# Two operands of a Mamba layer's gating moved into PSUM: the conv's Tanh, and y up to its gate

## The reference

```python
proj = h @ in_proj_w.T                       # h: layernorm(x)
gate, xBC, dt = split(proj, [INTER, INTER + CONV_DIM])
xBC = silu(causal_conv4(xBC) + conv_b)       # 4 taps, one filter per channel
x, Bm, Cm = split(xBC)
y = ssd(x, Bm, Cm, dt) + x * D               # mixing of tokens by C.B * decay, and the skip term
yg = y * silu(gate)
out = rmsnorm_by_group(yg) * norm_w @ out_proj_w.T
```

## Time and profile before

| | |
|---|---|
| median of 3 runs | 1576.83 us |
| the profiled execution's own time | 1575.93 us |
| its span, first to last instruction | 1573.70 us |
| mean granted TensorE clock | 0.993 of full speed |
| PE busy | 1529.4 us, 97% |
| DVE busy | 1367.7 us, 87% |
| POOL busy | 1045.9 us, 66% |
| ACT busy | 1010.5 us, 64% |

### The profile page before, as it was taken

One profiled execution on the slowest core, in us unless ns is written; L12 is line 12 of the kernel. 1 busy time (PEld: TensorE's weight loads), 2 busy tenths in 40 slices (PEclk: granted clock), 3 DMA queues, 4 the chain that ended last, 5 costly groups with the idle time before them and its releaser, 6 DMA issues. The chain is left out here.

```text
span 1573.7 us, 24488 instructions
## 1 busy us (share of the span) xinstructions
PE 1529.4 (97%) x8296; PEld 1229.0 (78%) x8296; DVE 1367.7 (87%) x1676; ACT 1010.5 (64%) x2126; POOL 1045.9 (66%) x789
## 2 busy tenths in 40 slices
PE   6978999999999999999999999999999999999988
PEld 4766788788888888788888888788888888788766
DVE  6679988998889988998889988998889988998674
ACT  4467766667666667667666667666666677567641
POOL 3026887588757887588757887488757886588740
PEclk9989999999999999999999999999999999999999
DMA  3033332223222232233222332223223322222101
GB/s 122 1 105 110 101 95 75 84 92 95 86 71 93 94 95 74 81 94 96 81 74 95 95 95 74 81 94 95 81 75 94 94 95 74 81 94 81 59 17 53
DMA packets 73514, 131.62 MB, mean 84 GB/s; under 512 B 10800, under 2 KB 10800, under 8 KB 73136
## 3 DMA queue, kind: packets, MB, share of 16 engines
q1 hardware_dynamic: 73392, 130.07, 25.9%
HBM read 127.43 MB, written 2.62 MB: 83 GB/s over the span
## 5 line engine op out<-in xcount | busy, mean ns | idle before, releaser
L164 PE MATMUL bank<-h_hi,mx_w_hi 128*128 128x512 f32 x1152 | 457.5, 397 | 5.1 <-DVE mx_xd L1480 4.0
L166 PE MATMUL bank<-h_hi,mx_w_lo 128*128 128x512 f32 x1152 | 449.5, 390 | 0.0
L165 PE MATMUL bank<-h_lo,mx_w_hi 128*128 128x512 f32 x1152 | 448.4, 389 | 0.0
L970 DVE SCALAR_TENSOR_TENSOR mx_acc<-bank,mx_cw,mx_acc 128x510 f32<-128x510 f32 (+2 forms) x480 | 353.7, 745 | 55.4 <-ACT mx_acc L955 43.9
L1289 ACT ACTIVATE mx_mix<-mx_csb,ncs 128x256 f32<-128x256 f32 x512 | 217.9, 497 | 138.5 <-PE bank L1679 138.5
L1473 DVE TENSOR_TENSOR mx_mix<-mx_mix,mx_cbt 128x1536 f32<-128x1536 f32 x128 | 280.5, 2196 | 2.5 <-ACT mx_mix L1299 2.5
L917 POOL TENSOR_TENSOR mx_w_lo<-mx_w_raw,mx_w_hi 128x512 fp32r<-128x512 f32 x144 | 213.8, 1501 | 74.3 <-ACT mx_w_hi L912 74.1
L164 PEld LDWEIGHTS bank<-h_hi,mx_w_hi 128*128 128x128 f32 x1152 | 216.5, 188 | 50.9 <-issue 8.7
L166 PEld LDWEIGHTS bank<-h_hi,mx_w_lo 128*128 128x128 f32 x1152 | 216.3, 188 | 46.3
L1200 POOL TENSOR_TENSOR mx_ssum<-mx_ssum,mx_sq 128x512 f32<-128x512 f32 x112 | 216.3, 1954 | 51.5 <-ACT mx_sq L1321 51.5
L165 PEld LDWEIGHTS bank<-h_lo,mx_w_hi 128*128 128x128 f32 x1152 | 216.7, 188 | 42.7
(11 more groups left out here) (171 smaller groups left out, 2132.6 us busy)
## 6 DMA issues: line engine op xcount, KB each, us to landing
mx_csb<-cs_rows SPq DMA_DIRECT2D x128, 512.0 KB, 3.9
mx_w_raw<-in_w_in SPq DMA_DIRECT2D x144, 256.0 KB, 2.9
mx_wo_raw<-in_w_out SPq DMA_DIRECT2D x64, 256.0 KB, 4.1
res<-in_x SPq DMA_DIRECT2D x8, 256.0 KB, 4.8
out<-res SPq DMA_DIRECT2D x8, 256.0 KB, 2.0
f_base_raw<-in_base_wt SPq DMA_DIRECT2D x1, 1024.0 KB, 7.4
mx_acc<-in_base_wt SPq DMA_DIRECT2D x1, 1024.0 KB, 4.8
cs_rows<-f_xn SPq DMA_DIRECT2D x2, 256.0 KB, 2.0
```

The lines of the kernel that those rows point to most:

```text
L164: nc.tensor.matmul(out, w_hi, x_hi, start=first, stop=False)
L165: nc.tensor.matmul(out, w_hi, x_lo, start=False, stop=False)
L166: return nc.tensor.matmul(out, w_lo, x_hi, start=False, stop=last)
L970: self.nc.vector.scalar_tensor_tensor(dst, src[:, :, 0:SEQ - k], self.cw[:, c, TAPS - 1 - k:TAPS - k], dst, ALU.mult, ALU.add).then_inc(s[ ...
```

## The change

1. `tanh_conv` writes its result into the projection's own bank (`m.bank[u % 2]`), no longer into the SBUF tile `th`, except for units 2 and 3; `silu_conv` reads it there. So the bank is in use until `silu_conv` of the unit is done, and `ip.project` waits on `conv` where it waited on `tap` (for units 0 to 3 and 6 onward; units 4 and 5, which follow 2 and 3, still wait on `tap`).
2. `skip_y` leaves its sum in `Y_BANK`. `gate_y` moves from POOL to DVE: it reads the bank and `sg` and writes `y` to SBUF, behind both `skip_y` of a pair. The mixing two steps later, and the next group's `b_dot_c`, wait on `yg` (gate done) where they waited on `ysb` (sum done). The wait on `ylo` (the old `y` row read) goes from `skip_y` to `gate_y`.
3. `keep_bc` of groups 1 to 7 moves from DVE to ACT, and in ACT's tail `decay_from_second(g + 1, 1)` goes behind `tanh_conv(g + 1, 5)`.

```diff
@@ InProj.project
         if not (first(g) and u < 2):
-            pe.wait_ge(s["tap"], 1 + (TAPS - 1) * (UNITS * g + u - 1))
+            if 4 <= u < 6 or (first(g) and u < 4):
+                pe.wait_ge(s["tap"], 1 + (TAPS - 1) * (UNITS * g + u - 1))
+            else:
+                pe.wait_ge(s["conv"], 1 + UNITS * g + u - 1)
@@ mixer_phase
+        def tanh_place(u):
+
+            return m.bank[u % 2][:, :] if u < 2 or u >= 4 else th[:, u % 2, :]
@@ gpsimd
-            def gate_y(g, st):
-                pool.wait_ge(s["ysb"], 1 + STEPS * g + st + 1)
-                pool.wait_ge(s["sg"], 1 + STEPS * g + st + 1)
-                nc.gpsimd.tensor_tensor(y[:, st, :], y[:, st, :], sg[:, st % 2, :], ALU.mult).then_inc(s["yg"], 1)
...
-                    for st in before:
-                        gate_y(g, st)
...
-                gate_y(g, STEPS - 2)
-                gate_y(g, STEPS - 1)
-                if more:
                     remainder_w(WPG * (g + 1) + 3)
@@ scalar
-                nc.scalar.activation(th[:, u % 2, :], acc[:, u % 4, :, :].rearrange("p b t -> p (b t)"),
+                nc.scalar.activation(tanh_place(u), acc[:, u % 4, :, :].rearrange("p b t -> p (b t)"),
                                      ACT.Tanh).then_inc(s["th"], 1)
...
                     evacuate(g + 1, 4)
+                    keep_bc(g + 1, 0)
                     decay_from_first(g + 1, 1)
                     evacuate(g + 1, 5)
                     tanh_conv(g + 1, 4)
-                    decay_from_second(g + 1, 1)
                     round_tile(g + 1, 1)
                     tanh_conv(g + 1, 5)
+                    decay_from_second(g + 1, 1)
+                    keep_bc(g + 1, 1)
@@ vector
-                nc.vector.scalar_tensor_tensor(a, th[:, u % 2, :], 1.0, a, ALU.add, ALU.mult).then_inc(s["conv"], 1)
+                nc.vector.scalar_tensor_tensor(a, tanh_place(u), 1.0, a, ALU.add, ALU.mult).then_inc(s["conv"], 1)
...
-                nc.vector.scalar_tensor_tensor(y[:, st, :], x, dh[:, j:j + 1], Y_BANK[i][:, :],
-                                               ALU.mult, ALU.add).then_inc(s["ysb"], 1)
+                nc.vector.scalar_tensor_tensor(Y_BANK[i][:, :], x, dh[:, j:j + 1], Y_BANK[i][:, :],
+                                               ALU.mult, ALU.add).then_inc(s["ysb"], 1)
+
+            def gate_y(g, st):
+                dve.wait_ge(s["ysb"], 1 + STEPS * g + st + 1)
+                dve.wait_ge(s["sg"], 1 + STEPS * g + st + 1)
+                dve.wait_ge(s["ylo"], 1 + STEPS * g + (XT if st >= XT else 0))
+                nc.vector.tensor_tensor(y[:, st, :], Y_BANK[st % 2][:, :], sg[:, st % 2, :],
+                                        ALU.mult).then_inc(s["yg"], 1)
...
-                    skip_y(g, a - 2)
-                    skip_y(g, a - 1)
+                    for st in (a - 2, a - 1):
+                        skip_y(g, st)
+                    for st in (a - 2, a - 1):
+                        gate_y(g, st)
...
-                    keep_bc(g + 1, 0)
-                    keep_bc(g + 1, 1)
@@ tensor, b_dot_c
-                    pe.wait_ge(s["ysb"], 1 + STEPS * g)
+                    pe.wait_ge(s["yg"], 1 + STEPS * g)
@@ tensor, mix_tokens
-                    pe.wait_ge(s["ysb"], 1 + STEPS * g + st - 1)
+                    pe.wait_ge(s["yg"], 1 + STEPS * g + st - 1)
```

More of the change, by code:

```diff
@@ L1161, in _ @@
         def _(pool):
-            start_at_one(pool, [s["yg"], s["ssum"], s["masked0"], s["masked1"]])
+            start_at_one(pool, [s["ssum"], s["masked0"], s["masked1"]])
             start_after_quad(pool, [s["ylo"]])
@@ L1260, in _ @@
         def _(act):
-            start_at_one(act, [s["tg"], s["decay"], s["sq"], s["wohi"], s["gcopy"], s["root"]])
+            start_at_one(act, [s["cbt"], s["tg"], s["decay"], s["sq"], s["wohi"], s["gcopy"], s["root"]])
             start_after_quad(act, [s["yhi"]])
@@ L1337, in round_w, with keep_bc @@
                     ip.round_w(act, *weight(n))
-            def keep_bc(hf):
-                act.wait_ge(s["cb"], 1 + hf + 1)
+            def keep_bc(g, hf):
+                act.wait_ge(s["cb"], 1 + 2 * g + hf + 1)
+                act.wait_ge(s["mix"], 1 + STEPS * g)
                 banks = Y_BANK if hf == 0 else O_BANK
@@ L1347, in _ @@
             tanh_conv(0, 2)
-            keep_bc(0)
+            keep_bc(0, 0)
             round_w(3)
@@ L1357, in _ @@
             tanh_conv(0, 5)
-            keep_bc(1)
+            keep_bc(0, 1)
             decay_from_first(0, 1)
@@ L1443, in _ @@
         def _(dve):
-            start_at_one(dve, [s["mix"], s["xd"], s["sg"], s["ysb"], s["cbt"],
+            start_at_one(dve, [s["mix"], s["xd"], s["sg"], s["ysb"], s["yg"],
                                s["ms"], s["inv"], s["wolo"]])
@@ L1488, in skip_y @@
                 dve.wait_ge(s["y"], 1 + STEPS * g + st + 1)
+                x = acc[:, st % 4, :, :].rearrange("p b t -> p (b t)")
+                nc.vector.scalar_tensor_tensor(Y_BANK[i][:, :], x, dh[:, j:j + 1], Y_BANK[i][:, :],
[3 more added lines that the diff above has]
+                dve.wait_ge(s["sg"], 1 + STEPS * g + st + 1)
                 dve.wait_ge(s["ylo"], 1 + STEPS * g + (XT if st >= XT else 0))
-                x = acc[:, st % 4, :, :].rearrange("p b t -> p (b t)")
-                nc.vector.scalar_tensor_tensor(y[:, st, :], x, dh[:, j:j + 1], Y_BANK[i][:, :],
-                                               ALU.mult, ALU.add).then_inc(s["ysb"], 1)
+                nc.vector.tensor_tensor(y[:, st, :], Y_BANK[st % 2][:, :], sg[:, st % 2, :],
+                                        ALU.mult).then_inc(s["yg"], 1)
             def silu_gate(g, st):
@@ L1571, in tail @@
             def tail(g, more):
-                skip_y(g, STEPS - 2)
-                skip_y(g, STEPS - 1)
+                for st in (STEPS - 2, STEPS - 1):
+                    skip_y(g, st)
+                for st in (STEPS - 2, STEPS - 1):
+                    gate_y(g, st)
                 if more:
```

## The result

The changed kernel takes 1590.24 us (median of 4 runs, 1586.18 to 1591.44) against 1577.05 us before: a ratio of 1.0078 with a 95% interval of 1.0063 to 1.0093. The same kernel timed a second time gave 1588.21 us against 1576.81, 1.0074 [1.0061, 1.0087]. So it is slower by 11 to 13 us, where 10.7 were forecast. The profiled execution after took 1586.18 us, span 1584.3.

The account below looks back on a forecast made before the run. PE alone was taken to bound groups 1 to 7, DVE the start of group 0. Terms 10.2 + 0 + 0.5 = 10.7 us on 1575.93 gave 1586.6 us, or 1587.5 against the median 1576.83; range 1580 to 1596.

Parts of the forecast that it names:

- The bound: Groups 1 to 7: PE alone sets the time, busy 176.56 of 177.00 us; relief of DVE or POOL pays nothing.
- The tails: Seven tails: project 6 waits 1.15 us for `silu_conv` of unit 4, plus 0.3 from ACT's copies; 10.2 us in all.
- The chain of 3.9 us: Tail: from PE's unit 5, evacuation, three taps, `silu_conv` and hand-over need 3.9 us against PE's 2.85 of other work.
- Group 0: Mixer's start: project(0, 6) starts 2.9 us late, at 110.05, repaid by about 1 us a pair over three pairs; net 0.
- DVE's relief: Rival, 9%: DVE was the hidden bound; 156 us saved in `silu_conv` against 87 us of gates gives 1566.6 us.
- The cover for the gates: Pairs of groups 1 to 7: 1.4 us of gates ahead of `scale_x` hide in 5.0 us of cover, costing PE nothing.
- The mixer's end: Last two steps: gates on DVE stand behind the second sum, delaying the rounding for the last projections; +0.5 us.
- The sum: Whole kernel: tails 10.2, group 0 0 and mixer's end 0.5 add 10.7 us; forecast 77%.
- stay at 1.78: Rival, 6%: `silu_conv` stays at 1.78 us because the bank takes part in the disturbance; costs 22.4 us, giving 1599 us.
- The clock: Rival, 8%: group 0's longer wait brings back the lower TensorE clock for 7.6 us, costing 3.8 us; 1591 us.
- That sign: Whole kernel after 100 us: a granted clock below 1.00 there would show the forecast wrong.

Follow-up runs that it names:

- part 1 alone: Kernel before with tanh in the bank and project waiting for `silu_conv`; gate stays on POOL, `keep_bc` on DVE: 1585.05 us, ratio 1.0052.
- parts 2 and 3 alone: Changed kernel with every conv's tanh back in the SBUF tile and every project waiting on `tap`: 1580.26 us, ratio 1.0015.
- the last version: Changed kernel with units 4 and 5 through SBUF, last pair's `scale_x` ahead of the gates, final gates each behind its own sum: 1574.95 us, ratio 0.9988.

## Why the prediction came out right, step by step

**The bound.** PE alone in groups 1 to 7: right. 199 us less on POOL and 53 less on DVE gave none of these groups a shorter period; the idle time of PE in a tail was paid in full.

**The tails.** Forecast 1.45 each, 10.2 in all; measured 1.42 and 9.9. Both terms were sized right: a tail costs 1.14 us with ACT as before (part 1 alone) where 1.15 stood, and 0.28 more for ACT's copies where 0.3 stood. `silu_conv` from a bank took 678 ns, forecast 0.68 us. The chain of 3.9 us, by which nothing could hide the delay, holds only in this order on DVE: with `silu_conv` of unit 4 ahead of the taps of unit 5, project 6 waited for nothing.

The Trainium skill, page "VectorE: DVE Perf Modes", section "The TRN2 errata — SBUF-src ops pay a fixed extra latency per instruction", gives 120 fixed cycles for a PSUM source against 58 for SBUF, an estimated 65 ns more for an operand in a bank. The measured 678 ns against 679 at best from SBUF do not show that; leaving it out was right.

**Group 0.** Forecast: 2.9 us late and repaid, net 0. The project started at 110.49, and at 110.26 in the second profile, forecast 110.05. The net was +0.5 in the profile with a low stretch near 130 us, -0.9 in the second profile without one (187.14 against 188.08). Right, within the bounds given. That it was repaid is DVE's relief: without the stall the same stretch gains 2.7 to 3.0 us (185.36 and 185.06). The relief is the shorter `silu_conv`: with parts 2 and 3 alone, where there is no stall either but the tanh stays in SBUF, it takes 188.81 us, against 186.10 in the version with units 4 and 5 through SBUF; in both the clock fell once more near 127 us.

**The cover for the gates.** Right for every pair but one. The step was "So this costs PE nothing", read from the middle pair of the earlier trace rows, where the cover is two projects. The last pair of the last group has no projects, and paid 1.2 us. A term that the prediction lacked. With `scale_x` ahead of the gates in that pair its wait was 0.52 us again, so the gates are shown as its cause.

**The mixer's end.** +0.5 forecast, 1.8 against 1.3 us of waits measured.

**The sum.** 10.7 forecast for the profiled execution, 10.25 measured (1575.93 to 1586.18). This closeness is partly luck: the change itself costs 11.7 us between the posts, and the end, where the execution before had a low stretch and the one after had none, gave 1.2 back, as much as the lacked term. Against the medians of the two comparisons the forecast is 0.7 and 2.5 us low: 11.4 and 13.2 us measured, in which the longer runs had the lower mean clock.

**The rivals.** DVE's relief did come, though smaller than reckoned from the median: all `silu_conv` together fell from 229.2 to 115.1 us, 114 less where 156 stood. It paid at group 0 alone. `silu_conv` did not stay at 1.78. The clock remains open in part: I wrote that I would be wrong if it fell below 1.00 after 100 us, and in the profile after it did, at 128 to 133 us, behind waits of 3.12, 1.09 and 0.57 us. That sign could not decide, since the kernel before also fell to the lower level, at 1544 us. And of five profiles with a group 0 wait of 2.6 us or more it fell between 110 and 137 us in two (this one, and part 1 alone), and of the five without (before among them) also in two (units 4 and 5 through SBUF, and parts 2 and 3 alone), so the long wait is not shown to cause it. The Trainium skill, page "TensorE: Matmul & The Clock Gate", section "Part 1: The HAM clock gate (the "warmup" mystery)", has throttling as the default and lets activity release it, from which the prediction took that the waits in the tails do no harm. The trace agrees: granted clock 1.00 from 635 to 812 us, with a wait of 1.17 in it. The runs of the changed kernel reach up to 1591.8 us, 5 us over its shortest, where before spread over 3 us in the same comparison. The long wait is not needed for that: the last version, without it, spreads over 5 us as well, from 1571.78 at a mean clock of 0.994 to 1576.81 at 0.991. What makes the clock fall in some executions and not in others stays open.

## What to carry over

When a buffer is made to live longer, look up who fills it next and where the new releasing instruction stands in its engine's order: here one instruction that stood behind four others it did not need cost a dense engine, with two copies on another engine, 1.42 us seven times, and exempting two of twenty units gave it all back. A cover read in a typical iteration must be read again in the first and the last, where the covering work may not exist. Moving work between engines that are not the bound pays only when it removes a wait of the one that is.

## What the runs showed of the hardware

- A tanh of 128x512 by ACT took 587 ns into a bank and 626 into SBUF (medians, changed kernel).
- `skip_y` took 755 ns with its sum in the bank, 745 with it in SBUF.
- `silu_conv` with one operand in a bank took 676 to 693 ns in all 142 cases; the 16 of the changed kernel with both operands in SBUF took 683 to 1633 (median 1044), the 158 of the kernel before 679 to 1821.
- A low stretch of the granted clock costs this kernel some 1.2 to 2.0 us: the part behind the last post took 71.63 us (`keep_bc` back on DVE) and 72.05 (the changed kernel) in profiles without any, 73.29 with one (before) and 75.24 with two (`silu_conv` of unit 4 first). Where it falls differs between executions of the same code: before, it fell behind waits of 1.44 and 0.63 us at 1541.80 and 1543.09, and not behind the same two waits of the changed kernel at 1553.60 and 1554.89. So two profiles are compared part by part, with the granted clock of each part beside it.
